# Cross-attention with layer norm on one core: padded last key tile, last output tile by column halves, an earlier mask, fewer warm-ups and work moved between engines

## What is computed

```python
Q = (x @ Wq), K = (ctx @ Wk), V = (ctx @ Wv)   # per head: 8 heads of 512
attn = softmax(where(mask, Q K^T / sqrt(512), -inf))
out = (attn V as rows of 8*512) @ Wo + x
return (out - mean) * rsqrt(var + 1e-5) * gamma + beta
```

## Time and profile before

| | |
|---|---|
| median of 3 runs | 374.01 us (373.94 to 374.32) |
| the profiled execution | 374.21 us |
| its span in the profile | 372.4 us |
| mean granted TensorE clock | 0.993 |
| busy: PE, DVE, POOL, ACT | 360.4, 288.5, 217.8, 210.2 us |

### The profile page before, as it was taken

The page is one execution under the profiler, slowest core; times in us unless marked ns, Lnnn a source line. Parts: engine busy times, 40 slices in busy tenths (PEclk is TensorE's granted clock), DMA queues, the critical chain, the costliest instruction groups (busy, mean ns, idle before and its releaser), DMA issues.

```text
span 372.4 us, 6736 instructions
## 1 busy us (share of the span) xinstructions
PE 360.4 (97%) x2354; PEld 334.6 (90%) x2354; DVE 288.5 (77%) x469; ACT 210.2 (56%) x742; POOL 217.8 (58%) x193
## 2 busy tenths in 40 slices
PE   8999999998999999999999999999999999999991
PEld 5999999998999998998899889988998999899880
DVE  0399999998878587777776877787778777877796
ACT  2567667766776566644664466446545654564610
POOL 0335535634447112777677767766776677677555
PEclk9999999999999999999999999999999999999997
DMA  8997679874732310414223143143241440411012
GB/s 266 425 394 278 225 279 341 346 266 154 282 113 101 129 56 2 132 42 169 84 87 141 58 142 131 41 171 89 83 141 65 134 143 30 169 73 42 31 57 84
DMA packets 19538, 55.81 MB, mean 150 GB/s; under 512 B 1712, under 2 KB 2992, under 8 KB 17584
## 3 DMA queue, kind: packets, MB, share of 16 engines
q1 hardware_dynamic: 18928, 54.59, 41.1%
q10 hardware_dynamic: 576, 0.79, 0.6%
HBM read 46.98 MB, written 8.39 MB: 149 GB/s over the span
## 4 chain that ended last, share of the span: by engine, by line
PE 82%; DVE 8%; POOL 3%; DMA 3%; ACT 2%; issue 1%; SPq 1%; POOLq 0%
PE pair L413 28%; PE pair L439 26%; PE pair L313 22%; PE pair L425 4%; DVE w_out_lo L621 3%; DMA w_proj<-wk 3%; PE pair L398 1%; POOL out_sb L804 1%; DVE mask_bias L614 1%; DVE kv_t L646 1%; ACT prob L552 1%; POOL var_eps L793 1%; DVE rest L642 1%; ACT w_out_hi L514 1%; POOL centred L800 1%
## 5 line engine op out<-in xcount | busy, mean ns | idle before, releaser
L552 ACT ACTIVATE prob<-masked,neg_max 128x77 f32<-128x77 f32 x256 | 88.3, 348 | 100.3 <-DVE neg_max L686 100.3
L809 POOL TENSOR_TENSOR w_proj_lo<-w_proj,w_proj_hi 128x768 fp32r<-128x768 f32 x28 | 51.9, 1877 | 61.0 <-ACT w_proj_hi L506 61.0
L313 PE MATMUL pair<-kv_t,w_out_hi 128*128 128x308 f32 x240 | 62.8, 335 | 1.0 <-DVE w_out_lo L621 1.0
L439 PE MATMUL pair<-vw_hi,pt_hi 128*128 128x512 f32 (+1 forms) x160 | 63.2, 395 | 0.0
L439 PE MATMUL pair<-vw_lo,pt_hi 128*128 128x512 f32 (+1 forms) x160 | 63.2, 395 | 0.0
L439 PE MATMUL pair<-vw_hi,pt_lo 128*128 128x512 f32 (+1 forms) x160 | 62.6, 391 | 0.0
L413 PE MATMUL pair<-a_hi,xt_hi 128*128 128x308 f32 x256 | 59.5, 314 | 0.0
L793 POOL TENSOR_SCALAR var_eps<-mean_var 128x1 f32<-128x1 f32 x32 | 24.2, 758 | 58.7 <-DVE mean_var L724 58.4
L413 PE MATMUL pair<-a_lo,xt_hi 128*128 128x308 f32 x256 | 57.1, 305 | 0.0
L413 PE MATMUL pair<-a_hi,xt_lo 128*128 128x308 f32 x256 | 57.0, 304 | 0.0
L786 POOL TENSOR_TENSOR xt_lo<-xt_in,xt_hi 128x512 fp32r<-128x512 f32 x32 | 44.0, 1377 | 20.6 <-ACT xt_hi L544 20.6
(11 more groups left out here) (59 smaller groups left out, 678.4 us busy)
## 6 DMA issues: line engine op xcount, KB each, us to landing
w_out<-wo SPq DMA_DIRECT2D x8, 1024.0 KB, 4.8
xt_in<-x_tiles SPq DMA_DIRECT2D x16, 512.0 KB, 3.9
x_in<-x_rows SPq DMA_DIRECT2D x16, 512.0 KB, 4.4
out<-out_sb SPq DMA_DIRECT2D x32, 256.0 KB, 2.1
w_out<-wq_t SPq DMA_DIRECT2D x7, 1024.0 KB, 5.7
w_proj<-wv SPq DMA_DIRECT2D x8, 768.0 KB, 5.2
w_proj<-wk SPq DMA_DIRECT2D x6, 768.0 KB, 8.1
w_out<-wq_t SPq DMA_DIRECT2D x2, 512.0 KB, 7.6
```

Source lines behind the costliest of these rows:

```text
L313: mm = pe.matmul(pair[:, bank, 0:n], w[:, m, k, :], moving[:, k, 0:n], start=(at == 0), stop=(at == len(steps) - 1))
L439: mm = pe.matmul(ps_out[:, i % 2, 0:s.model], ps[0:rows, j, :], v[0:rows, b, j, :], start=(j == 0 and n == 0), stop=(j == s.key_t - 1 and ...
L552: e = act.activation(prob[i % 2][:, cols], masked[i % 2][:, cols], ACT.Exp, bias=neg_max[i % 2][:, h:h + 1], accum_out=sums[i % 2][:, h:h ...
L809: pool.tensor_tensor(half_cols(w_proj_lo[u % W_RING], half), half_cols(w_proj_sb[u % W_RING], half), half_cols(w_proj_hi[u % 2], half).bit ...
```

## The change

Seven things are altered.

1. WARM_UP is 7 instead of 10.
2. The mask is loaded by ACT between the first and second weights, and its bias is computed by DVE right behind ctx's remainder.
3. DVE makes the remainders of the third weights (`split_first_rounded`), before use 0's product is taken out; POOL starts with the fourth.
4. SP issues the second w_out load only once PE has finished half of the first projection. Everything behind it in SP's list comes after it, as before.
5. The last key tile has 128 rows in `out_rows`: rows 96 to 127 of the last tile of vw_hi and vw_lo are set to zero at the start by four DVE memsets, rows 96 to 103 are then overwritten with data. The probabilities of rows 104 to 127 are whatever ps_pt holds. `split_pt` becomes one instruction on ACT and one on DVE.
6. For all tiles DVE makes var_eps (twice buffered), POOL rstd, ACT scales the centred tile, and POOL adds beta.
7. The last tile's output is computed by two halves of 256 columns, the second into a bank of the scores; residual and statistics follow by halves, the aggregation takes both, and the final scaling, the addition and the store go by halves too, the second store from ACT's queue.

```diff
+PAD_FROM = 96
...
-    WARM_UP = 10
+    WARM_UP = 7
...
+        pt_blocks = ps_pt[:, :, :].rearrange("p a n -> p (a n)")[:, 0:s.key_t * P]\
+            .rearrange("p (j q) -> p j q", q=P)
...
+        LAST = T - 1
+        COLS = s.model // 2
+
+        def last_cols(half):
+
+            return ps_out[:, LAST % 2, 0:COLS] if half == 0 else ps_scores[(LAST - 1) % 2][:, 0, 0:COLS]
...
                 if u + 1 < USES:
                     load_w_proj(u + 1)
+                if u == 1:
+                    sp.wait_ge(pe_proj, 1)
                 load_w_out(u)
                 if u == H:
-                    sp.dma_start(mask_sb[:, :], mask.rearrange("b k -> (b k)").partition_broadcast(P))\
-                      .then_inc(ld_mask, DMA_INC)
...
+                if t == LAST:
+                    sp.wait_ge(dve_last, 1)
+                    sp.dma_start(out[t * P:(t + 1) * P, 0:COLS], out_sb[t % OUT_RING][:, 0:COLS])\
+                      .then_inc(stored[t % OUT_RING], DMA_INC)
...
                 for j in range(s.key_t):
-                    rows = s.key_rows(j)
                     for n, (ps, v) in enumerate(passes):
-                        mm = pe.matmul(ps_out[:, i % 2, 0:s.model], ps[0:rows, j, :], v[0:rows, b, j, :],
+                        mm = pe.matmul(ps_out[:, i % 2, 0:s.model], ps[:, j, :], v[:, b, j, :],
...
+            def last_out_rows():
+                b = LAST // s.per_batch
+                pe.wait_ge(dve_pt_lo, LAST + 1)
+                pe.wait_ge(dve_resid, LAST - 1)
+                pe.wait_ge(dve_masked, LAST)
+                hi, lo = pt_hi[LAST % 2], pt_lo[LAST % 2]
+                passes = [(hi, vw_hi), (hi, vw_lo), (lo, vw_hi)]
+                for half in range(2):
+                    cols = slice(half * COLS, (half + 1) * COLS)
+                    for j in range(s.key_t):
+                        for n, (ps, v) in enumerate(passes):
+                            mm = pe.matmul(last_cols(half), ps[:, j, :], v[:, b, j, cols],
+                                           start=(j == 0 and n == 0),
+                                           stop=(j == s.key_t - 1 and n == len(passes) - 1))
+                    mm.then_inc(pe_last, 1)
...
+                if ld is ld_first:
+                    act.dma_start(mask_sb[:, :], mask.rearrange("b k -> (b k)").partition_broadcast(P))\
+                       .then_inc(ld_mask, DMA_INC)
...
+                act.activation(pt_hi[i % 2][:, :, :], pt_blocks, ACT.Copy).then_inc(act_pt_hi, 1)
+
+
+            def scale(i):
+                c = centred[i % 2][:, :]
+                act.wait_ge(pool_rstd, i + 1)
+                act.wait_ge(dve_centred, i + 1)
+                act.activation(c, c, ACT.Copy, scale=rstd[i % 2][:, 0:1]).then_inc(act_scaled, 1)
...
                 exps(i)
                 split_pt(i - 1)
+                if 3 <= i < T - 1:
+                    scale(i - 3)
             split_pt(T - 1)
+            scale(T - 4)
+            scale(T - 3)
+            scale(T - 2)
+            act.wait_ge(dve_last, 2)
+            act.dma_start(out[LAST * P:T * P, COLS:s.model], out_sb[LAST % OUT_RING][:, COLS:s.model])\
+               .then_inc(stored_last, DMA_INC)
...
             dve.memset(zeros[:, :], 0.0).then_inc(dve_zero, 1)
+            for v in (vw_hi, vw_lo):
+                for b in range(s.batches):
+                    dve.memset(v[PAD_FROM:P, b, s.key_t - 1, :].bitcast(F32), 0.0).then_inc(dve_pad, 1)
...
+            def split_first_rounded():
+                u = FULL_PROJ
+                for half in range(2):
+                    dve.wait_ge(act_p_hi, half + 1)
+                    dve.tensor_tensor(half_cols(w_proj_lo[u % W_RING], half), half_cols(w_proj_sb[u % W_RING], half),
+                                      half_cols(w_proj_hi[u % 2], half).bitcast(F32), ALU.subtract)\
+                       .then_inc(dve_p_lo, 1)
...
+            def centre(i):
+                y, mv = resid[:, :], mean_var[i % 2]
+                dve.wait_ge(dve_mv, i + 1)
                 if i >= 2:
+                    dve.wait_ge(pool_rstd, i - 1)
+                dve.tensor_scalar(var_eps[i % 2][:, :], mv[:, 1:2], EPS, None, ALU.add).then_inc(dve_ve, 1)
+                if 2 <= i < LAST:
                     dve.wait_ge(pool_out, i - 1)
...
+            def last_residual():
+                c = LAST // CHUNK
+                dve.wait_ge(ld_x[c % X_RING], use(c, X_RING))
+                dve.wait_ge(dve_centred, LAST)
+                for half in range(2):
+                    cols = slice(half * COLS, (half + 1) * COLS)
+                    dve.wait_ge(pe_last, half + 1)
+                    dve.tensor_tensor(resid[:, cols], last_cols(half), x_in[c % X_RING][:, LAST % CHUNK, cols], ALU.add)\
+                       .then_inc(dve_resid, 1)
+                    dve.wait_ge(dve_resid, LAST + half + 1)
+                    dve.bn_stats(stats_last[:, half, :], resid[:, cols]).then_inc(dve_stats, 1)
+                dve.wait_ge(dve_stats, LAST + 2)
+                dve.bn_aggr(mean_var[LAST % 2][:, :], stats_last[:, :, :]).then_inc(dve_mv, 1)
+                centre(LAST)
+                dve.wait_ge(pool_rstd, T)
+                dve.wait_ge(dve_centred, T)
+                last = LAST % OUT_RING
+                dve.wait_ge(stored[last], DMA_INC * (LAST // OUT_RING))
+                for half in range(2):
+                    cols = slice(half * COLS, (half + 1) * COLS)
+                    dve.scalar_tensor_tensor(out=out_sb[last][:, cols], in0=centred[LAST % 2][:, cols],
+                                             scalar=rstd[LAST % 2][:, 0:1], in1=beta_sb[:, cols], op0=ALU.mult,
+                                             op1=ALU.add).then_inc(dve_last, 1)
...
             split_ctx()
+            bias_of_mask()
             for u in range(USES):
                 if u + 1 < USES:
                     split_kv(u + 1)
-                if u == H + 1:
-                    bias_of_mask()
+                if u + 2 == FULL_PROJ:
+                    split_first_rounded()
...
+            def inverse_deviation(i):
+                pool.wait_ge(dve_ve, i + 1)
+                if i >= 2:
+                    pool.wait_ge(act_scaled, i - 1)
+                pool.tensor_tensor(rstd[i % 2][:, :], var_eps[i % 2][:, :], minus_half[:, :], ALU.pow).then_inc(pool_rstd, 1)
+
+            def shift(i):
+                pool.wait_ge(act_scaled, i + 1)
                 if i >= OUT_RING:
                     pool.wait_ge(stored[i % OUT_RING], DMA_INC * (i // OUT_RING))
-                pool.wait_ge(pool_scaled, i + 1)
-                pool.tensor_tensor(o, c, beta_sb[:, :], ALU.add).then_inc(pool_out, 1)
-
-            for u in range(FULL_PROJ, USES):
+                pool.tensor_tensor(out_sb[i % OUT_RING][:, :], centred[i % 2][:, :], beta_sb[:, :], ALU.add)\
+                    .then_inc(pool_out, 1)
+
+            for u in range(FULL_PROJ + 1, USES):
```

More of the change, by code:

```diff
@@ L158, in build @@
         out_sb = [sb(f"out_sb{n}", [P, s.model]) for n in range(OUT_RING)]
+        var_eps = [var_eps0, sb("var_eps1", [P, 1])]
+        rstd = [rstd0, sb("rstd1", [P, 1])]
+        stats_last = sb("stats_last", [P, 2, 6])
         pairs = [stack.enter_context(nc.psum_tensor(f"pair{n}", [P, 2, 512], F32)) for n in range(4)]
@@ L488, in _ @@
             out_rows(T - 2)
[L489 removed]
+            last_out_rows()
         @block.scalar
@@ L763, in _ @@
             residual(T - 2)
-            residual(T - 1)
-            dve.wait_ge(pool_rstd, T)
-            dve.wait_ge(dve_centred, T)
-            last = (T - 1) % OUT_RING
-            dve.wait_ge(stored[last], DMA_INC * ((T - 1) // OUT_RING))
-            dve.scalar_tensor_tensor(out=out_sb[last][:, :], in0=centred[(T - 1) % 2][:, :], scalar=rstd[:, 0:1],
-                                     in1=beta_sb[:, :], op0=ALU.mult, op1=ALU.add).then_inc(dve_last, 1)
+            last_residual()
         @block.gpsimd
```

77 lines of the change are left out of this document (34 added, 43 removed).

## The result

The changed kernel takes 370.65 us (370.46 to 370.87) against 373.98 us (373.61 to 374.32) for the kernel before, four runs of each on one chip: a ratio of 0.9911, 95% interval 0.9894 to 0.9929. The profiled execution took 370.46 us for a span of 368.7 us, at a mean granted clock of 0.998; the span before was 372.4. So 3.3 us went by the medians and 3.7 by the spans, where 4.4 was forecast.

The account below looks back on a forecast made before the run. PE, busy 360.4 of 372.4 us, was taken as the bound, so only the ends and gaps could shrink. Start 0.9, gaps 1.5 and tail 2.0 sum to 4.4 us: 374.01 - 4.4 = 369.6 us, range 367.8 to 371.3.

Parts of the forecast that it names:

- prediction's own signs: Trace marks listed beforehand across start, gaps, middle and tail; a w_out rounding later than 16.3 us would refute the forecast.
- Start: Up to PE's first rounded projection: fewer warm-ups and DVE's remainders bring it from 16.53 to about 15.6, gain 0.9 us.
- costed at nothing: At the start: the mask load (77 KB, 0.2 us), its bias operations and the padding memsets were taken as covered.
- The warm-ups' 0.64 us: At the start: three warm-ups fewer free 1.28 us, filled by real matmuls at half rate, gain 0.64 us.
- The load held back: SP's second w_out load, issued at about 6.5 us, still lands at 15.95; 0.4 us of cover.
- Rival A: At the start: the held-back load lands 2.0 us later, at 17.95, and the time is 371.2 us; 10%.
- Gaps: PE's 0.97 and 0.95 us waits at 84 and 88 us shrink to one of 0.44; gain 1.5 us, from 1.2 to 2.0.
- Middle: The tiles where PE is always busy: work moved among ACT, DVE and POOL is covered by PE, gain zero.
- the 128-row term: Last key tile's matmuls at 128 rows: 395 ns against 397 for 104, so zero, 0.2 us less at most over 32 tiles.
- Tail: After PE's last tile: output by halves and scaling off POOL end DVE earlier; gain 2.0 us, ends 1.0 and 2.8.
- rival C: The tail doesn't shrink because the weight load holds the 256-column matmuls, 1.9 us more; 371.5 us; 5%.
- Rivals B and D: At the start: the clock rises a few us later, 371.6 us, 9%; or stays low through the unrounded stage, 379.4, 3%.

Follow-up runs that it names:

- e2_mask_rows: Changed kernel with the mask loaded from an array holding it 128 times, so each row has its own address; 369.63 us, ratio 0.9885.
- e10_mask_alone: Kernel before with only the mask's load moved behind the first weights and its bias operations to VectorE's start; 373.34 us, ratio 0.9989.
- e9: Changed kernel with the remainders of the third weights back on POOL; 371.55 us, ratio 0.9935.
- e4: Changed kernel with ten warm-up matmuls again instead of seven; 370.63 us, ratio 0.9911.
- e3_no_hold: Changed kernel without SP's wait for PE before the second w_out load; 370.65 us, ratio 0.9913.
- e8: Changed kernel with 104 rows again in the last key tile's matmuls for tiles 0 to 30; 371.02 us, ratio 0.9924.
- e5: Changed kernel with the last tile in one piece again: 512-column matmuls, one residual, one output, one store; 370.68 us, ratio 0.9916.
- e7: Changed kernel with the last tile's two low-part passes left out, 10 matmuls instead of 30, output incomplete; 370.54 us, ratio 0.9912.
- e11: Changed kernel with the last tile's first-half residual and statistics ahead of tile 30's centring on DVE, in their own buffer; 371.04 us, ratio 0.9922.
- e1_mask_last: Changed kernel with the mask's load issued by ACT behind both parts of the second weights; 370.16 us, ratio 0.9899.

## Why the prediction was right, and where it was not

The forecast was 369.6 us with a range of 367.8 to 371.3, and 370.65 lies in it, 1.05 above. The sum was 0.9 + 1.5 + 2.0 = 4.4; by the spans it is 0.35 + 1.7 + 0.35 + 1.1 + 0.2 = 3.7. Two terms were too large, by some 1.4 us together (start and tail), and three were too small, by some 0.75 (gaps, middle and store). That the total is as near as it is owes something to luck. Of the prediction's own signs three failed: w_out was first rounded at 16.72, where later than 16.3 was to make the forecast wrong; the first rounded projection came at 16.32 and not near 15.6; and DVE ended 4.46 us behind PE, not 3.3.

**Start: 0.9 predicted, 0.35 measured.** The step that failed is the sentence on what is "costed at nothing": it priced the mask's load by its bytes, 77 KB, at 0.2 us. Its price is that of 128 reads of one address: the rate at 85 and 184 GB/s for two microseconds, third weights 0.8 us late (14.23 against 13.40 in e2_mask_rows), 1.06 us of PE in e10_mask_alone, and 0.7 in the product's time (19.43 against 18.73). With own addresses the paragraph's times hold: 13.43, 15.6 and 0.9 predicted, 13.40, 15.59 and 1.05 measured. DVE's remainder was sized right, 0.96 us a half for 0.95, and e9 puts its worth at 0.9 us or more. The bias operations took 0.24 and 1.44 us, not 1.04 and 2.98 us; POOL is idle beside them here, where before a subtraction of its own ran from 77.75 to 81.43. The warm-ups' 0.64 us was not cashed in the changed kernel: the loads bound the start with them or without (e4). In e2_mask_rows, where they don't, PE's second set of unrounded matmuls starts at 11.49 in place of 11.77, so 0.28 us of it is seen.

**The load held back.** The prediction left its landing unchanged. It moved from 15.95 to 16.7, but through the mask's load: it is 15.88 in e2_mask_rows, with the hold in place, and 16.78 in e3_no_hold, without it. Rival A, the load late by its delay, is out.

**Gaps: 1.5 predicted, 1.7 measured** (1.74 in e10_mask_alone). The first stop is gone, and 0.45 us is left of the second as forecast. The brackets give 0.97 + 0.95 - 0.45 = 1.47. The other 0.24 is in the same two places, as the starts show (1.12 for 0.97 and 0.59 for 0.50): the brackets understate what a stop costs.

**Middle: zero predicted, 0.4 measured.** The scaling on ACT hides as said: no PE wait from 140 to 330 us. What was mis-sized is the 128-row term, "below zero by 0.2 us at most". The mean lengths (395 and 397 ns) are lengths of overlapping records and hid it; e8 measured 13 ns a tile. PE's last tile gives 0.06 back (3.69 us from its first matmul to its last end, 3.63 before), which leaves the 0.35 of the sum.

**Tail: 2.0 predicted; 1.1 behind PE's end and 0.2 at the store measured.** The 2.0 were 2.3 behind PE's end (DVE ending 3.25 us behind PE where it was 5.57) less 0.3 that PE's last tile was to take longer. Three steps failed.
First, "DVE's own chain on the tile before ends at 364.2 (POOL is a step behind it and no longer scales)", half a microsecond before PE's end. It ended 0.1 after it, a loss of 0.6 us; 0.47 of that is the centring, which met POOL's addition and took 1.21 for 0.74. The low end of 1.0 had such a collision in it, the forecast had not.
Second, the inverse deviation at 0.57 beside the centring. It waited 0.27 us for POOL's addition and took 1.00, and ended at 365.49. From the end of var_eps (364.22) to DVE's output (365.52) it is 1.3 us, where the prediction had 0.8: another 0.5 us.
Third, the halves were to give the overlap. They gave nothing (e5), because it is not PE that is waited for (e7). The first two make up 1.1 of the 1.2 us that are missing behind PE's end. PE's last tile was over-priced, 0.06 us longer than before and not 0.3, with the weight load holding nothing: rival C is out.

**Why 0.57 was the wrong row.** POOL's inverse deviation takes 0.99 where DVE runs a centring beside it (mean 988 ns of 32 in the changed kernel), and 0.54 where DVE is idle (the last one in e11). The rows of before showed 0.57, but there POOL spent 0.54 to 0.78 us on var_eps first, beside the centring, and the inverse deviation came after it. A duration goes with its neighbours, and the change moved the neighbours. The Trainium skill ("SBUF — State Buffer", SBUF: two separate sides) says that VectorE and GpSimd share a pair of ports that one of them holds for a whole instruction, and that a VectorE operation with two SBUF inputs is among those that take it. The traces agree: DVE's centring started at 360.83 beside an addition that ran until 361.49, and ended 0.55 later. With the 0.6 and the 0.5 us in the sum the forecast would have been 370.7, an estimate from this case's rows, and it would have been near for a wrong reason still, as the start was 0.55 too good.

**Rivals B and D.** The clock rose about when it did before (24 matmuls in 3.80 us for 3.42 at the full rate) and stayed up. The moment varies between traces of the same start, and it hardly counts: the 24 matmuls took 3.39 us in e8_rows104 and 4.37 in e7_short_last, and the product stood at 19.28 and 19.54.

## What to carry to other kernels

A load that broadcasts one row to 128 partitions is not priced by its bytes: keep it out of the time in which other loads bound the kernel, or give it rows of its own (here worth 1.0 us). Where a step is moved to another engine, take the duration of each operation from a row that has the neighbours it will have, above all for DVE and POOL. And before splitting work to overlap with an engine, check that the engine is what the tail waits for: here a version with 2.3 us less of it took as long.

## What was not expected of the hardware

- 128 rows of 616 bytes from one address: DMA at 85 and 184 GB/s for two microseconds with loads queued; from 128 addresses 334 and 376.
- TensorE's rise to the full rate came at different times though the start of the program was the same. The warm-ups run 0.425 us per 512 columns (1.2 GHz) while the page's granted clock already reads 1.00, so the rise has to be read from the matmuls: in e10_mask_alone ten warm-ups take 3.79 us and not 4.45, so it is before 5 us; in e1_mask_last the count of matmuls is still 6 and 7 in the microseconds from 5 and from 6, and 10 from 7 on. It did not set e1's start: PE's first rounded matmul at 16.13 comes 0.26 us behind DVE's remainder of the late third weights, as it does in the changed kernel (16.32 behind 16.06).
- Matmuls of 128 rows are faster than the same columns at 104 rows: with three of a tile's fifteen changed, a tile is 13 to 16 ns shorter.
